# Rotary halves moved by DMA, keys and values in one product, and a scan that starts one tile earlier beside the feed-forward layer

## The chip, the core and the metric

The kernel runs on one core of a Trainium2 chip. The metric is the time of one execution on the device, in microseconds (us). A core has five engines that run their own instruction streams and meet through semaphores: PE (matrix products; its weight loads are shown as PEld), DVE (vector work), ACT (activations, and it can issue DMAs), POOL (here it issues accumulating DMAs) and SP (it issues DMAs and nothing else). 16 DMA engines serve all queues.

## The reference

One decoder layer for 4 batches of 512 positions by 512 features, all in float32: attention with 16 query heads over 2 key/value heads, then a state-space block (Mamba) on a context of 256 features whose output is gated by the layer-normed x, then a feed-forward layer with 8 experts' low-rank adapters, 2 picked per position.

```python
q = rope((x @ wq.T + bq).reshape(b, l, 16, 32)); k = rope((x @ wk.T + bk).reshape(b, l, 2, 32))
v = (x @ wv.T + bv).reshape(b, l, 2, 32)
# rope: x1, x2 = halves of a head's 32; [x1*cos - x2*sin, x2*cos + x1*sin]
x = x + softmax(causal(q @ k.T * scale)) @ v @ wo.T          # x was layer-normed
xi = silu(conv4(in_proj(ctx)) + conv_b)                      # 512 channels
dt_low, B, C = split(x_proj(xi)); dt = softplus(dt_proj(dt_low) + dt_b)
for l in positions:                                          # 16 states per channel
    state = state * exp(dt[l] * A) + dt[l] * xi[l] * B[l];  y[l] = state @ C[l]
x = x + (y + D * xi) * silu(layernorm(x))
# feed-forward, 1408 wide: base product, and the same with each picked expert's adapters
h0 = silu(g) * u;  hk = silu(g + g_lora_k) * (u + u_lora_k);  out = h0 @ Wd.T + sum_k w_k * (hk @ Ad_k.T @ Bd_k.T)
```

## The kernel before, in words

Features or channels lie on the 128 partitions and positions along the row, 512 wide, so a channel block is one 128x512 tile. The batches are a software pipeline: while PE computes the feed-forward layer of batch t, DVE and ACT run the scan of batch t+1, and the attention of t+1 follows. All orders are written out in the program; each engine runs its block (`@block.tensor`, `@block.vector`, ...) as one stream. A pass over one batch has these stages:

- **Head**: output of attention, gate, normalisation, router, masks; beside them the convolution of the next batch and its x-projection (`project_x`, L711), which ACT copies to xdt_sb (`split_first`, L508) and stores to DRAM as bc_rows, the rows of B and C. ACT then starts y_sb with D*u (L516).
- **Evaluations** (33 of them, `EVAL`): for each of 11 tiles f of the feed-forward width a base product (`base`, L858: eight 128x512 products) and two adapter steps (`add_slot`, L870), each followed by ACT's silu (L642) and DVE's product with the up half (L1211), then `down_adapters` (L878). The small products that make dt (`project_dt`, L720) and their softplus (L522) sit beside evaluations 2 and 3 (`DT_SLOTS`); the normalisation of the next batch's x (L982, L992) sits at evaluations 1 and 3 (`NORM_AT`).
- **Down stage** (11 slots): the down product (L938, four 128x512 products a slot) on PE, and beside it the projections of the next batch (`project`). Query tile n is projected at slot n+1 (L746), moved by ACT to q_raw (L570), turned by a product with a constant matrix (`rot`, L753), and DVE forms raw*cos + turned*sin in three instructions (`rotate`, L1054, L1057, L1061) at slot n+2. Tile 4 is the keys, stored once for each of four row groups. The values come after it, by four products of their own (L760), an ACT move (L576), four transposes (L767) and one copy (L1066).
- **Attention** (32 steps, L784 on PE: two heads by 128 queries a step).

The scan of one batch is cut in 49 pieces on DVE (`scan_piece`): "du", and for each of 16 states "mul" (L1035), "run" (the scan itself, L1040) and "out" (L1045), all over 128x2048. A table (`plan`) deals them to slots: 29 pieces in the evaluations, 20 in the down stage, none in the attention of batches 1 to 3. For each state ACT makes a decay (`make_decay`, L548, four exponentials), ACT issues the broadcast load bc_sb (L538), and POOL adds the result to y_sb by a DMA (L461). Decays and B/C rows are double buffered, so state n waits for state n-2. q_raw is double buffered as well: ACT moves tile n only when DVE has finished tile n-2.

Batch 0 has no feed-forward layer beside it: its projections run alone, with one scan piece in each of 11 slots, and the rest of its scan lies in its attention.

## Time and profile before

| | us |
|---|---|
| median of 3 runs | 1518.23 (1510.87 to 1524.1) |
| the profiled execution | 1524.03, its span 1522.2 |
| PE busy | 1368.4 (90%) |
| DVE busy | 1021.4 (67%) |
| ACT busy | 701.7 (46%) |

The span is what the trace covers; the profiled execution's own time is 1.8 us longer. A pass over a batch in the middle repeats every 351.6 us, three times. Busy shares are means over stages that have different limits, so the sections below read single stretches. In rows of the trace a number in brackets is the time in which the engine stood idle just before, with what it waited for; "issue" there means that the trace shows no wait. Matmul rows count two records for one float32 product.

### The profile page before, as it was taken

The numbers are of one execution on the slowest core, as the hardware profiler recorded it, in microseconds if no ns is written. First come the engines' busy times: TensorE is split into PE (matmuls) and PEld (weight loads), VectorE is DVE, ScalarE is ACT, GpSimd is POOL, SyncE is SP. The second block draws the span as 40 slices with busy tenths as digits, with TensorE's granted clock in tenths as the row PEclk, the third lists the DMA queues.
The fourth block names the chain that finished last, engine by engine and source line by source line (L and its number), as shares of the span: only waits on it lengthen the run. The fifth ranks groups of instructions, "written<-read, shape, count | busy, mean of one in ns | idle before, by whom it ended". The sixth has DMA issues, their size and how long they took to land.

```text
span 1522.2 us, 15997 instructions
## 1 busy us (share of the span) xinstructions
PE 1368.4 (90%) x5768; PEld 673.0 (44%) x5768; DVE 1021.4 (67%) x1203; ACT 701.7 (46%) x1490; POOL 89.6 (6%) x116
## 2 busy tenths in 40 slices
PE   6747777999999899899999799899999799799999
PEld 2324444444444465444444365444444355444443
DVE  4799996578989645669898744748988944511110
ACT  5445653365542385365552276455553177211110
POOL 0000001000000000000000000100000000100000
PEclk8955569999999699999999689999999879699999
DMA  5376661147767600127766700126766620011202
GB/s 200 70 191 147 137 141 31 41 121 176 187 151 170 152 2 2 44 72 183 186 162 156 188 11 2 42 64 151 188 162 159 154 67 2 0 31 52 62 31 83
DMA packets 53277, 158.80 MB, mean 104 GB/s; under 512 B 5072, under 2 KB 10704, under 8 KB 44752
## 3 DMA queue, kind: packets, MB, share of 16 engines
q0 software_dynamic: 9216, 67.11, 22.1%
q1 hardware_dynamic: 25664, 54.23, 10.8%
q10 hardware_dynamic: 18320, 36.45, 8.5%
q8 instruction: 47, 0.77, 0.2%
q14 instruction: 30, 0.25, 0.0%
HBM read 86.20 MB, written 4.46 MB: 60 GB/s over the span
## 4 chain that ended last, share of the span: by engine, by line
PE 66%; DVE 21%; ACT 6%; issue 4%; DMA 3%; ACTq 0%; DVEq 0%; POOL 0%
PE ps_a L858 21%; PE ps_a L870 9%; DVE state L1040 8%; PE ps_a L938 5%; PE ps_b L878 5%; PE ps_a L784 5%; PE ps_w L837 4%; PE ps_b L798 3%; DVE state L1035 3%; PE ps_w L746 3%; DMA y_sb<-state 3%; DVE state L1045 3%; PE ps_w L904 2%; ACT r L590 2%; DVE neg_max L1075 2%
## 5 line engine op out<-in xcount | busy, mean ns | idle before, releaser
L858 PE MATMUL ps_a<-xt,w_sb 128*128 128x512 f32 x704 | 320.0, 609 | 6.4 <-DVE r L1211 6.4
L1040 DVE TENSOR_TENSOR_SCAN state<-decay,state 128x2048 f32<-128x2048 f32 x64 | 282.7, 4417 | 2.1
L1211 DVE TENSOR_TENSOR r<-r,ps_a 128x512 f32<-128x512 f32 x132 | 90.2, 685 | 189.3 <-ACT r L642 189.3
L858 PEld LDWEIGHTS ps_a<-xt,w_sb 128*128 128x128 f32 x704 | 137.0, 196 | 180.8 <-issue 180.8
L642 ACT ACTIVATE r<-ps_a 128x512 f32<-128x512 f32 x132 | 78.4, 596 | 268.2 <-PE ps_a L858 122.7
L590 ACT ACTIVATE r<-ps_a,neg_max 128x128 f32<-128x128 f32 (+3 forms) x256 | 134.1, 539 | 121.4 <-DVE neg_max L1075 116.0
L784 PE MATMUL ps_a<-r 32*128 32x512 f32 (+3 forms) x512 | 137.0, 620 | 51.6 <-ACT r L590 34.2
L548 ACT ACTIVATE decay<-dt_sb,decay_rate 128x511 f32<-128x511 f32 x256 | 163.2, 710 | 18.3 <-DVE state L1040 17.9
L870 PE MATMUL ps_a<-r,wb_sb 128*128 128x512 f32 x352 | 166.2, 595 | 4.5 <-DVE r L1211 2.2
L938 PE MATMUL ps_a<-wd_sb,r 128*128 128x512 f32 x352 | 163.3, 616 | 0.0
L1035 DVE TENSOR_TENSOR state<-du_sb,bc_sb 128x2048 f32<-128x2048 f32 x64 | 146.1, 2283 | 9.0 <-DMA bc_sb<-bc_rows 5.2
L1045 DVE TENSOR_TENSOR state<-state,bc_sb 128x2048 f32<-128x2048 f32 x64 | 146.4, 2287 | 1.7
L1075 DVE TENSOR_REDUCE neg_max<-ps_a 128x2 f32<-128x256 f32 (+3 forms) x128 | 104.7, 819 | 44.3 <-PE ps_a L787 42.3
L798 PE MATMUL ps_b<-cst,r 128*128 128x128 f32 x640 | 117.1, 325 | 15.2 <-ACT r L602 7.8
L938 PEld LDWEIGHTS ps_a<-wd_sb,r 128*128 128x128 f32 x352 | 70.5, 201 | 89.0 <-issue 86.0
L870 PEld LDWEIGHTS ps_a<-r,wb_sb 128*128 128x128 f32 x352 | 66.3, 190 | 90.2 <-issue 85.1
L461 POOL DMA_DIRECT2D y_sb<-state x64 | 55.8, 873 | 748.6 <-DVE state L1045 668.1
L798 PEld LDWEIGHTS ps_b<-cst,r 128*128 128x128 f32 x640 | 87.5, 171 | 22.1 <-issue 18.6
L878 PE MATMUL ps_b<-r,ad_sb 128*128 128x512 f32 x176 | 87.6, 622 | 2.9 <-DVE r L1211 2.9
L784 PEld LDWEIGHTS ps_a<-r 32*128 32x128 f32 x512 | 49.4, 235 | 85.7 <-ACT r L590 46.5
L1088 DVE TENSOR_TENSOR r<-ps_w,r 128x128 f32<-128x128 f32 x64 | 18.4, 287 | 78.1 <-ACT r L609 78.1
L602 ACT ACTIVATE xt<-ps_b 128x256 f32<-128x256 f32 (+1 forms) x128 | 57.9, 504 | 24.0 <-PE ps_b L798 23.4
(117 smaller groups left out, 1392.9 us busy)
## 6 DMA issues: line engine op xcount, KB each, us to landing
y_sb<-state POOLq DMA_DIRECT2D x64, 1024.0 KB, 9.5
bc_sb<-bc_rows ACTq DMA_DIRECT2D x64, 512.0 KB, 5.4
w_sb<-in_w_tiles SPq DMA_DIRECT2D x44, 512.0 KB, 8.0
wd_sb<-in_w_down SPq DMA_DIRECT2D x44, 256.0 KB, 3.2
wb_sb<-in_w_adapt SPq DMA_DIRECT2D x44, 128.0 KB, 2.1
xa<-in_x SPq DMA_DIRECT2D x4, 1024.0 KB, 5.2
out_x<-xb SPq DMA_DIRECT2D x16, 256.0 KB, 8.1
xn_att<-in_ctx_t SPq DMA_DIRECT2D x4, 512.0 KB, 7.8
```

The costliest lines, as they stand in the source:

```text
L548: nc.scalar.activation(decay[:, n % 2, j, 1:L], dt_sb[:, j, 1:L], ACT.Exp, scale=decay_rate[:, j, n:n + 1]).then_inc(decay_ready, 1)
L590: nc.scalar.activation(probs[:, (2 * s + k) % 4, 0:(i + 1) * P], score_place(s, k), ACT.Exp, bias=neg_max[:, s % 2, k:k + 1], accum_out=ro ...
L784: nc.tensor.matmul(score_place(s, k), q_t[rows, m, i * P:(i + 1) * P], k_t[rows, 0:width], start=True, stop=False, tile_position=(rows.sta ...
L798: mm = nc.tensor.transpose(ps_b[:, k, kt * P:(kt + 1) * P], probs[:, (2 * s + k) % 4, kt * P:(kt + 1) * P], ident)
L858: mm = nc.tensor.matmul(ps_a[:, 2 * (f % 2) + half, :], w_sb[:, slot, at + k * P:at + (k + 1) * P], xt[:, k, :], start=(k == 0), stop=Fals ...
L870: mm = nc.tensor.matmul(ps_a[:, 2 * (f % 2) + half, :], wb_sb[:, f % 2, at:at + P], low[:, 2 * half + k - 1, :], start=False, stop=(k == 2 ...
L878: mm = nc.tensor.matmul(ps_b[:, k - 1, :], ad_sb[:, f, :], hk[:, (2 * f + k - 1) % 4, :], start=(f == 0), stop=(f == FT - 1), skip_group_c ...
L938: mm = nc.tensor.matmul(ps_a[:, i, :], hb[:, f, i * P:(i + 1) * P], wd_sb[:, f % 2, :], start=(f == 0), stop=False, skip_group_check=True)
L1035: tt(state[:, n % 2, :, :], du_sb[:], row, ALU.mult).then_inc(scan_chain, 1)
L1040: nc.vector.tensor_tensor_scan(flat, decay[:, n % 2, :, :].rearrange("p j l -> p (j l)"), flat, 0.0, ALU.mult, ALU.add).then_inc(scan_chai ...
L1045: tt(state[:, n % 2, :, :], state[:, n % 2, :, :], row, ALU.mult).then_inc(scan_chain, 1)
L1075: nc.vector.tensor_reduce(neg_max[:, s % 2, :], both, AX.X, ALU.max, negate=True)\
```

## The change

Two things change together.

**Keys, values and rotation.** The constant matrix and its five products go. After ACT has moved a tile to q_raw, SP issues eight DMAs of 16 rows each that write its swapped halves to q_rot (`rotate` in SP's block), and the table of sines now carries the sign. Keys and values come from one product, tile 0 (wkv_sb, rows of keys and values in turn); the queries are tiles 1 to 4. The key rows are copied to their second places by two DMAs. The four value transposes follow at slot 3 and DVE copies the values out in four instructions at slot 4. The four value products and ACT's move of them go.

**The scan.** The dt products and softplus move from evaluations 2 and 3 to 0 and 1, "du" and "mul 0" from evaluation (1,1) to (0,1), and so every later piece of the evaluations by one tile. 32 pieces lie in the evaluations, 17 in the down stage. The start of y_sb moves from ACT to DVE (`begin_y`), the normalisation to evaluations 0, 1 and 3, and decay 0 is made at the slot of "du", behind the softplus.

```diff
-NORM_AT = {EVAL_AT[0, 1]: (0, 1), EVAL_AT[0, 2]: (2, 3)}
-DT_SLOTS = (2, 3)
+NORM_AT = {EVAL_AT[0, 0]: (0, 1), EVAL_AT[0, 1]: (2,), EVAL_AT[0, 2]: (3,)}
+DT_SLOTS = (0, 1)
...
-        slots[between(at["du", 0] if n < 2 else at["run", n - 2], at["run", n])]["decay"].append(n)
+        slots[at["du", 0] if n == 0 else between(at["du", 0] if n == 1 else at["run", n - 2], at["run", n])]["decay"].append(n)
...
-IN_EVALS = [0 if f == 0 else ((0, 2, 0) if f == 1 else (0, 2, 1))[k] for f, k in EVAL]
-IN_DOWN = 20
+IN_EVALS = [({EVAL_AT[0, 1]: 2}.get(e, 0) if f == 0 else (0, 2, 1)[k]) for e, (f, k) in enumerate(EVAL)]
+IN_DOWN = 17
...
+VALUES_AT = 3
+COPY_AT = 8
 def projections(f):
     raw = f - 1 if 1 <= f <= TILES else None
-    back = f - 2 if 2 <= f <= TILES + 1 else None
-    return raw, back, {TILES + 2: 0, TILES + 3: 1}.get(f)
+    turned = f - 2 if 2 <= f <= TILES + 1 else None
+    return raw, turned
...
+            raw = projections(f)[0]
+            names += [("raw", raw)] * (raw is not None) + [("vt", 0)] * (f == VALUES_AT)
...
+        q_rot = r2[:, 6:8, :]
...
+            def rotate(b, n):
+                bank, count = use(("raw", n), b)
+                sp.wait_ge(work_free[bank], count + 1)
+                for p in range(0, P, HD):
+                    for to, of in ((p, p + HD // 2), (p + HD // 2, p)):
+                        sp.dma_start(q_rot[to:to + HD // 2, n % 2, :], q_raw[of:of + HD // 2, n % 2, :])\
+                            .then_inc(rot_loaded[n % 2], 16)
+            def copy_keys(b):
+                sp.wait_ge(qk_ready, b * TILES + 1)
+                for p in (0, 2 * HD):
+                    sp.dma_start(k_t[p + HD:p + 2 * HD, :], k_t[p:p + HD, :]).then_inc(k_copied, 16)
+            def beside_down(b, f):
+                if 0 <= f - 3 < TILES:
+                    rotate(b, f - 3)
+                if f == COPY_AT:
+                    copy_keys(b)
             def ffn_loads(t):
                 for f in range(2, FT):
                     load_w(t, f)
                     load_wb(t, f)
                 for f in range(FT):
                     load_wd(t, f)
+                    if t + 1 < BATCH:
+                        beside_down(t + 1, f)
...
+            for n in range(TILES):
+                rotate(0, n)
+            copy_keys(0)
...
-                act.wait_ge(u_ready, b * JT + JT)
-                for j in range(JT):
-                    nc.scalar.activation(y_sb[:, j, :], u_sb[:, j, :], ACT.Identity,
-                                         scale=vec[:, V_D + j:V_D + j + 1]).then_inc(y_init, 1)
             def softplus(b, tiles):
...
-                        act.wait_ge(dt_ready, b + 1)
+                        for j in (JT - 2, JT - 1):
+                            bank, count = use(("dt", j), b)
+                            act.wait_ge(work_free[bank], count + 1)
...
+                    if n == 2:
+                        of, turned = use(("vt", 0), b)
+                        act.wait_ge(work_full[of], turned + 1)
+                    bias = q_bias[:, n - 1:n] if n > 0 else vec[:, V_BKV:V_BKV + 1]
                     nc.scalar.activation(q_raw[:, n % 2, :], ps_w[:, bank, :], ACT.Identity, bias=bias,
-                                         scale=SCALE if n < MT else 1.0).then_inc(work_free[bank], 1)
-                if projections(f)[2] == 0:
-                    act.wait_ge(v_full, b + 1)
-                    act.wait_ge(qk_ready, b * TILES + TILES)
-                    nc.scalar.activation(q_raw[:, 0, :], ps_b[:, 0, :], ACT.Identity,
-                                         bias=vec[:, V_BV:V_BV + 1]).then_inc(v_moved, 1)
+                                         scale=SCALE if n > 0 else 1.0).then_inc(work_free[bank], 1)
...
-            for f in range(FT):
-                if f == 0:
-                    transposed("att", "xt", 0, False)
+            load_bc(0, PLAN_FIRST[DOWN])
+            make_decay(0, PLAN_FIRST[DOWN])
+            transposed("att", "xt", 0, False)
+            project(0, 0)
+            for f in range(1, FT):
...
-                    scan_inputs(t + 1, PLAN_NEXT[e])
+                    load_bc(t + 1, PLAN_NEXT[e])
                     softplus(t + 1, [j for _, j in dt_uses(e)])
+                    make_decay(t + 1, PLAN_NEXT[e])
...
-                raw, back, values = projections(f)
+                raw = projections(f)[0]
                 if raw is not None:
                     if raw == 0:
                         xt_moved("xt", b, False)
                     bank = fill(pe, ("raw", raw), b)
                     for k in range(KT):
-                        w = wq_sb[:, k, raw * P:(raw + 1) * P] if raw < MT else wk_sb[:, k, :]
+                        w = wq_sb[:, k, (raw - 1) * P:raw * P] if raw > 0 else wkv_sb[:, k, :]
                         mm = nc.tensor.matmul(ps_w[:, bank, :], w, xt[:, k, :], start=(k == 0), stop=(k == KT - 1))
                     mm.then_inc(work_full[bank], 1)
-                if back is not None:
-                    bank = fill(pe, ("back", back), b)
-                    raw_bank, raw_count = use(("raw", back), b)
+                if f == VALUES_AT:
+                    raw_bank, raw_count = use(("raw", 0), b)
                     pe.wait_ge(work_free[raw_bank], raw_count + 1)
-                    nc.tensor.matmul(ps_w[:, bank, :], rot, q_raw[:, back % 2, :], start=True, stop=True)\
-                        .then_inc(work_full[bank], 1)
-                if values == 0:
-                    if not first_batch(b):
-                        pe.wait_ge(down_ready, b)
-                    for k in range(KT):
-                        mm = nc.tensor.matmul(ps_b[:, 0, :], wv_sb[:, k, :], xt[:, k, :],
-                                              start=(k == 0), stop=(k == KT - 1))
-                    mm.then_inc(v_full, 1)
-                if values == 1:
-                    pe.wait_ge(v_moved, b + 1)
+                    bank = fill(pe, ("vt", 0), b)
                     for i in range(NT):
-                        mm = nc.tensor.transpose(ps_b[:, 0, i * P:(i + 1) * P], q_raw[:, 0, i * P:(i + 1) * P], ident)
-                    mm.then_inc(v_turned, 1)
+                        mm = nc.tensor.transpose(ps_w[:, bank, i * P:(i + 1) * P], q_raw[:, 0, i * P:(i + 1) * P], ident)
+                    mm.then_inc(work_full[bank], 1)
             def attention(b, slots):
                 pe.wait_ge(qk_ready, (b + 1) * TILES)
-                pe.wait_ge(v_ready, b + 1)
+                pe.wait_ge(k_copied, 32 * (b + 1))
+                pe.wait_ge(v_ready, NT * (b + 1))
...
+            def begin_y(b):
+                dve.wait_ge(u_ready, b * JT + JT)
+                for j in range(JT):
+                    ts(y_sb[:, j, :], u_sb[:, j, :], vec[:, V_D + j:V_D + j + 1], None, ALU.mult).then_inc(y_init, 1)
+            def normalize_next(t, e):
+                for i in NORM_AT.get(e, ()):
+                    dve.wait_ge(loaded["x"], 16 * t + 32)
+                    deviation("att", t + 1, xa, i)
+                for i in NORM_AT.get(e, ()):
+                    scaled("att", t + 1, xa, xn_att, i)
...
-                total = TILES
-                _, n, values = projections(f)
+                n = projections(f)[1]
                 if n is not None:
                     raw_bank, raw_count = use(("raw", n), b)
                     dve.wait_ge(work_free[raw_bank], raw_count + 1)
                     tt(rope_tmp, q_raw[:, n % 2, :], cos_t, ALU.mult).then_inc(rope_chain, 1)
-                    bank = filled(dve, ("back", n), b)
-                    part = q_t[:, n, :] if n < MT else k_t
-                    tt(part, ps_w[:, bank, :], sin_t, ALU.mult).then_inc(work_free[bank], 1)
-                    dve.wait_ge(rope_chain, b * total + n + 1)
-                    bank, count = use(("back", n), b)
-                    dve.wait_ge(work_free[bank], count + 1)
+                    of_parity = (TILES + 1 - n % 2) // 2
+                    dve.wait_ge(rot_loaded[n % 2], 16 * 2 * (P // HD) * (b * of_parity + n // 2 + 1))
+                    part = q_t[:, n - 1, :] if n > 0 else k_t
+                    tt(part, q_rot[:, n % 2, :], sin_t, ALU.mult).then_inc(rope_chain, 1)
+                    dve.wait_ge(rope_chain, 2 * (b * TILES + n + 1))
                     tt(part, part, rope_tmp, ALU.add).then_inc(qk_ready, 1)
-                    dve.wait_ge(qk_ready, b * total + n + 1)
-                if values == 1:
-                    dve.wait_ge(v_turned, b + 1)
-                    nc.vector.tensor_copy(v_sb[:], ps_b[:, 0, :].rearrange("p (i d) -> p i d", i=NT)[:, :, 0:VD])\
-                        .then_inc(v_ready, 1)
+                    dve.wait_ge(qk_ready, b * TILES + n + 1)
+                if f == VALUES_AT + 1:
+                    bank = filled(dve, ("vt", 0), b)
+                    turned = ps_w[:, bank, :].rearrange("p (i g c d) -> p i g c d", i=NT, g=KV_HEADS, c=2)
+                    for i in range(NT):
+                        copied = nc.vector.tensor_copy(v_sb[:, i, :].rearrange("p (g d) -> p g d", g=KV_HEADS),
+                                                       turned[:, i, :, 1, :])
+                        copied.then_inc(v_ready, 1)
+                    dve.wait_ge(v_ready, NT * (b + 1))
+                    nc.vector.tensor_copy(scrap[:], ps_w[0:1, bank, 0:1]).then_inc(work_free[bank], 1)
...
             normalize("att", 0, xa, xn_att)
+            begin_y(0)
...
+                begin_y(t + 1)
+                normalize_next(t, 0)
                 for e in range(1, EVALS):
                     evaluate(t, e)
-                    for i in NORM_AT.get(e, ()):
-                        dve.wait_ge(loaded["x"], 16 * t + 32)
-                        deviation("att", t + 1, xa, i)
-                    for i in NORM_AT.get(e, ()):
-                        scaled("att", t + 1, xa, xn_att, i)
+                    normalize_next(t, e)
...
-    c[:, C_SIN:C_SIN + L] = np.sin(ang)
+    c[:, C_SIN:C_SIN + L] = np.where(p % HD < half, -1.0, 1.0).astype(np.float32)[:, None] * np.sin(ang)
...
+    def keys_values(k, v):
+        return np.concatenate([part[g * HD:(g + 1) * HD] for g in range(KV_HEADS) for part in (k, v)])
```

ACT, first evaluations of a batch in the middle, before (L508 the copy to xdt_sb, L516 the start of y_sb, L522 softplus, L548 decays, L642 the silu of an evaluation, r2 the gate):

```order
L508 ACTIVATE xdt_sb<-ps_b 128x512
L513 DMA bc_rows<-xdt_sb 32x512
L516 ACTIVATE y_sb<-state,vec 128x512 x4
L642 ACTIVATE r2<-ps_a 128x512 x2
L522 ACT_TABLE_LOAD
L522 ACTIVATE dt_sb<-ps_w,vec 128x512 x2
L642 ACT_TABLE_LOAD
L642 ACTIVATE r2<-ps_a 128x512
L522 ACT_TABLE_LOAD
L522 ACTIVATE dt_sb<-ps_w,vec 128x512 x2
L642 ACT_TABLE_LOAD
L642 ACTIVATE r2<-ps_a 128x512
```

And now (softplus is L542, decays L566, silu L657):

```order
L533 ACTIVATE xdt_sb<-ps_b 128x512
L538 DMA bc_rows<-xdt_sb 32x512
L542 ACT_TABLE_LOAD
L542 ACTIVATE dt_sb<-ps_w,vec 128x512 x2
L657 ACT_TABLE_LOAD
L657 ACTIVATE r2<-ps_a 128x512
L554 DMA bc_sb<-bc_rows 128x2x512 x2
L542 ACT_TABLE_LOAD
L542 ACTIVATE dt_sb<-ps_w,vec 128x512 x2
L566 ACT_TABLE_LOAD
L566 ACTIVATE decay<-dt_sb,decay_rate 128x511 x4
L657 ACT_TABLE_LOAD
```

The four instructions on y_sb are gone, softplus and the first decay stand between the first silus.

SP, the down stage of a batch in the middle, now (before, eleven rows of wd_sb stood there with nothing between):

```order
L412 DMA wd_sb<-in_w_down 128x512 x4
L419 DMA r2<-r2 16x512 x8
L412 DMA wd_sb<-in_w_down 128x512
L419 DMA r2<-r2 16x512 x8
L412 DMA wd_sb<-in_w_down 128x512
L419 DMA r2<-r2 16x512 x8
```

Each group of eight waits for ACT's move of its tile, and the weight loads behind it wait with it.

DVE, the start of the down stage, now (L1239 ends the weighing of the adapters, L1058 is the scan itself, L1063 and L1053 "out" and "mul", L1071 to L1077 the rotation):

```order
L1239 TENSOR_TENSOR r1<-r2 128x512
L1058 SCALAR_TENSOR_TENSOR state<-decay,state 128x2048
L1063 TENSOR_TENSOR state<-state,bc_sb 128x2048
L1053 TENSOR_TENSOR state<-du_sb,bc_sb 128x2048
L1071 TENSOR_TENSOR r2<-r2,cst 128x512
L1075 TENSOR_TENSOR r2<-r2,cst 128x512
L1077 TENSOR_TENSOR r2<-r2 128x512
L1058 SCALAR_TENSOR_TENSOR state<-decay,state 128x2048
L1063 TENSOR_TENSOR state<-state,bc_sb 128x2048
```

Three scan pieces instead of four stand ahead of the first rotation, and L1075 now waits for DMAs, where it waited for a product.

## Rows read from the trace of the kernel before

**Rows 1.** Busy time by stage, a middle batch: start:end, length, busy by engine, clock, DMA.
```profile
588.00:940.00 352.00, 329.67 (x1468) 162.12 (x1458) 256.22 (x300) 182.32 (x378) 22.34 (x28) 0.94 0.43 109
```

**Rows 2.** The chain of waits over the whole span: start us, us, what.
```profile
698.91 6.87 PE ps_a L858 x16
710.92 6.87 PE ps_a L858 x16
```

**Rows 3.** The chain of waits, end of the same batch's down stage.
```profile
860.68 1.21 DVE xb L1224 x2
862.03 0.79 PE ps_a L784 x4
```

**Rows 4.** Timeline of ACT, first evaluations: start us, us, what, idle before.
```profile
644.11 0.60 ACT L508 ACTIVATE xdt_sb<-ps_b 128x512 f32<-128x512 f32 x1 [6.19 <-PE ps_b L711]
645.18 2.56 ACT L516 ACTIVATE y_sb<-state,vec 128x512 f32<-128x512 f32 x4 [0.48 <-ACT xdt_sb L508]
...
655.57 1.26 ACT L522 ACTIVATE dt_sb<-ps_w,vec 128x512 f32<-128x512 f32 x2
...
669.30 2.56 ACT L548 ACTIVATE decay<-dt_sb,decay_rate 128x511 f32<-128x511 f32 x4
671.88 1.28 ACT L642 ACT_TABLE_LOAD   x1
673.17 1.08 ACT L642 ACTIVATE r<-ps_a 128x512 f32<-128x512 f32 x2
```

**Rows 5.** Timeline of PE, the same evaluations.
```profile
674.63 7.11 PE L858 MATMUL ps_a<-xt,w_sb 128*128 128x512 f32 x16 [2.13 <-DVE r L1211]
```

**Rows 6.** Timeline of DVE, the same evaluations.
```profile
648.25 0.69 DVE L1211 TENSOR_TENSOR r<-r,ps_a 128x512 f32<-128x512 f32 x1 [6.11 <-ACT r L642]
```

**Rows 7.** Timeline of DVE, the down stage.
```profile
783.18 0.69 DVE L1216 TENSOR_TENSOR r<-ps_b,r 128x512 f32<-128x512 f32 x1 [1.36 <-PE ps_b L878]
...
785.12 4.42 DVE L1040 TENSOR_TENSOR_SCAN state<-decay,state 128x2048 f32<-128x2048 f32 x1
789.57 2.29 DVE L1045 TENSOR_TENSOR state<-state,bc_sb 128x2048 f32<-128x2048 f32 x1
...
801.42 0.69 DVE L1057 TENSOR_TENSOR r<-ps_w,cst 128x512 f32<-128x512 f32 x1 [2.22 <-PE ps_w L753]
...
809.14 0.69 DVE L1057 TENSOR_TENSOR r<-ps_w,cst 128x512 f32<-128x512 f32 x1 [1.11 <-PE ps_w L753]
...
848.26 0.40 DVE L1066 COPY v_sb<-ps_b 128x256 f32<-128x256 f32 x1
...
851.51 2.29 DVE L1035 TENSOR_TENSOR state<-du_sb,bc_sb 128x2048 f32<-128x2048 f32 x1 [0.66 <-DMA y_sb<-state]
```

**Rows 8.** Timeline of PE, the down stage.
```profile
790.06 3.60 PE L746 MATMUL ps_w<-xt,wq_sb 128*128 128x512 f32 x8
...
842.82 1.11 PE L767 MATMUL ps_b<-cst,r 128*128 128x128 f32 x4 [3.68 <-ACT r L576]
```

**Rows 9.** DMA issues of the whole span: KB each, median us to landing.
```profile
y_sb<-state POOLq DMA_DIRECT2D x64, 1024.0 KB, 9.5
bc_sb<-bc_rows ACTq DMA_DIRECT2D x64, 512.0 KB, 5.4
wd_sb<-in_w_down SPq DMA_DIRECT2D x44, 256.0 KB, 3.2
...
bc_rows<-xdt_sb ACTq DMA_DIRECT2D x4, 64.0 KB, 1.6
```

**Rows 10.** SP's issues of line 410: duration of one in ns, min/median/max.
```profile
L410 SPq DMA_DIRECT2D wd_sb<-in_w_down x44: 327/328/433, 404.3 to 1508.7; - x44
```

**Rows 11.** Busy time, two groups of eight attention steps (columns of rows 1).
```profile
862.00:883.60 21.60, 21.32 (x114) 11.08 (x114) 8.46 (x18) 12.80 (x44) 0.00 (x0) 0.50 0.65 183
895.20:911.70 16.50, 15.98 (x208) 10.05 (x204) 8.24 (x21) 14.71 (x54) 0.00 (x0) 1.00 0.01 2
```

**Rows 12.** Timeline of DVE, batch 0, the first "mul".
```profile
43.92 2.29 DVE L1035 TENSOR_TENSOR state<-du_sb,bc_sb 128x2048 f32<-128x2048 f32 x1 [5.18 <-DMA bc_sb<-bc_rows]
```

More of the change, by code:

```diff
@@ L279, in decoder_layer @@
         qk_ready = sem("qk_ready")
-        v_full = sem("v_full")
-        v_moved = sem("v_moved")
-        v_turned = sem("v_turned")
+        rot_loaded = [sem(f"rot_loaded{k}") for k in range(2)]
+        k_copied = sem("k_copied")
         v_ready = sem("v_ready")
@@ L1280, in constant_table @@
     half = HD // 2
-    for m in range(P):
-        if m % HD < half:
-            c[m + half, C_ROT + m] = -1.0
-        else:
-            c[m - half, C_ROT + m] = 1.0
     c[:, C_MASK:C_MASK + P] = np.where(p[None, :] <= p[:, None], 0.0, NEG)
-    for k in range(32, P):
-        c[k, C_SEL + k % 32] = 1.0
     inv = (np.float32(10000.0) ** (-np.arange(half, dtype=np.float32) / np.float32(half))).astype(np.float32)
@@ L1343 @@
         "wq": rows(a["L0_attn_wq"][heads].T),
-        "wk": rows(a["L0_attn_wk"][kv_rows].T),
-        "wv": rows(np.tile(a["L0_attn_wv"].T, (1, P // VD))),
+        "wkv": rows(keys_values(a["L0_attn_wk"], a["L0_attn_wv"]).T),
         "wo": rows(a["L0_attn_wo"][:, heads].T),
```

31 lines of the change are left out of this document (10 added, 21 removed).

## The prediction, made before the changed kernel ran

> **What bounds the kernel now.** I read the windows by stage first, then the chain of waits, then the timelines of the engines where the chain changes hands. In a middle batch PE is busy 330 of 352 us and DVE 256 [rows 1]. The chain says where each of them counts. In the evaluations it is PE: the base product of one tile starts 12.01 us after that of the tile before [rows 2], which is 14 products at 6.87/8 = 0.86 us, with nothing between. In the down stage PE's own work is some 80 products, but the end is DVE's: its last scan piece ends at 860.7, the sums of the output follow, and only then does the first attention product start, at 862.03 [rows 3]. So a PE product taken out of the down stage is worth nothing by itself; a scan piece taken out is worth its duration, if DVE does not wait instead. Two PE stalls stand out: 2.13 us ahead of the third base product, for ACT and DVE [rows 5], and 3.68 us for the values' move [rows 8], which DVE's longer path hides. Attention starts at granted clock 0.50, which is 1.2 GHz, and later steps have 1.00, 2.4 GHz [rows 11].
>
> **The change, part by part.** I use the middle batch's times; batches 1 to 3 repeat it.
>
> *Evaluations.* After ACT's copy to xdt_sb ends at 644.7, it lost 2.56 us on y_sb [rows 4]. Now it goes: load 1.28, two softplus 1.26 (647.3), load, silu 0.60 (649.2), load, softplus (651.7), load 1.28, decay 2.56 (655.6), load (656.9) [rows 4]. PE meanwhile does two dt products, an adapter step, two dt products (0.86 each, 6 in all) and the base product of 6.87: 644.8 + 5.2 + 6.9 = 656.9. So the next silu is ready when its product is, and PE is not held. The second decay, which with its two table loads had kept the silu from PE (669.3 to 673.2 [rows 4]), now stands one tile earlier and behind three silus that are done by then, ahead of a base product of 6.87 us that covers its 1.28 + 2.56 + 1.28 = 5.1. The 2.13 us stall goes: -2.1 a batch; bounds +2 (a stall at the new place) and -2.9 (0.7 more for the dt products that fill PE's first wait). DVE takes four instructions for y_sb, at most 0.69 each by the nearest row, 2.8 in all, in a wait of 6.11 us [rows 6]; without that cover they would delay an evaluation by as much. The three more pieces lie in tiles 0 and 1, where DVE had only the evaluations. From tile 2 on both kernels have three pieces a tile: 4.42 + 2 x 2.25 plus three evaluations of 0.69 is 11.0 of 12.0 us, unchanged.
>
> A row shows 1.28 us for a table load, and the activation after it starts 0.01 us later [rows 4]. The Trainium skill (ScalarE: Activation LUTs, "What ACT_TABLE_LOAD costs") puts a switch at 2.66 us, with a drain of 1.38 behind the load. By it the silu above, behind five loads, would come 6.9 us later, and the evaluations would lose about 4.5 us a batch, not gain 2.1. The trace disagrees, so I don't use it.
>
> *Down stage, pieces.* 20 pieces (7 scans, 13 products) become 17 (6 and 11): 4.42 + 2 x 2.25 = -8.9 us on DVE's path [rows 7]. The values cost four small copies and a one-element copy where one of 0.40 was [rows 7]: +0.8 (between 0 and 1.6).
>
> *Down stage, waits.* DVE waited 2.22 + 1.11 + 0.66 = 4.0 us in the stage [rows 7]. The new wait is for the swapped halves. Let d be the time from ACT's move to their landing. SP issues eight, 0.33 to 0.43 us each [rows 10], so 2.6 to 3.5. A 64 KB DMA lands in 1.6, a 256 KB one on SP's own queue beside this stage's traffic in 3.2 [rows 9]. So d lies between 4.2 and 6.7; I take 2.9 + 2.4 = 5.3. Tile 0's product still ends at 793.7 [rows 8], its move at 794.3, the halves land at 799.6. DVE, after weighing (783.2 to 785.1) and three pieces (8.9), stands at the rotation at 794.7: it waits 4.9. Rotation 2: ACT moves tile 2 only after issuing the load of B and C for state 13, which waits for "out 11"; DVE then has a rotation, a "mul" and 0.65 to do (4.9), and ACT's move and d come to 6.8, so 1.9. Rotations 1, 3 and 4 have two or more pieces of cover. At the end, "mul 15" waits for POOL's addition of state 13, 9.5 us [rows 9], against 8.9 of DVE's work: 0.6. Together 7.4 instead of 4.0, +3.4. Sum of the stage: -8.9 + 0.8 + 3.4 = **-4.7**; with d = 4.2 it is -6.9, with d = 6.7 it is -1.9.
>
> *Down stage, PE and SP.* PE loses nine products (7.7 us) and its 3.68 wait, and is done near 843, twelve us before DVE: nothing. Weight loads for slots 4 to 8 now wait behind rotations; each is issued one to two slots (3.4 to 6.9 us) ahead of its use and lands in 3.2 [rows 9]: nothing, or under 1 us of PE time that DVE hides. The two key copies land before DVE is through.
>
> *Attention.* PE still idles ahead of it, so it starts at the lower clock as now: 0. *Last batch's feed-forward layer:* untouched.
>
> *Batch 0.* ACT's 2.56 us ahead of softplus go, and "mul 0" waited 5.18 us for rows that are now asked for earlier [rows 12]; against it, decay 0 (1.28 + 2.56) stands ahead of the moves of xt, and rotation 0 waits for d. I take -2.3, between 0 and -4.
>
> Sum: 3 x (-2.1 - 4.7) - 2.3 = **-22.7 us**. The profiled execution is 1524.0, so 1501.3 for one like it; it is the slowest of the three, and against the median of 1518.2 the forecast is 1495.5, rounded to **1496 us**.
>
> **The rivals.**
>
> *The eight DMAs land one after the other (slower).* Then d = 8 x 1.6 = 12.8 [rows 9]. Rotations 0, 2 and 4 wait 12.4, 9.4 and 4.9, with 0.6 at the end 27.3: the stage becomes 15 us longer, a batch 13; with +6 in batch 0 the time is 1518 + 39 + 6 = 1563. It decides from d of about 9. For it: they are small, on one queue, and share the engines with POOL's additions. Against it: SP's issue times [rows 10] don't show one waiting for the last. The Trainium skill (DMA: Bandwidth & Descriptors, "Rules for kernel authors") speaks for it: transfers to disjoint groups of partitions serialize, and those under 64 KB are mostly overhead. Chance 0.08.
>
> *The traffic slows them part of the way.* d = 8: waits of 7.4, 4.4 and 0.6 eat what the three pieces give, the evaluations' 2.1 stays: 1518 - 6 = 1512. The spread of landings on SP's queue speaks for some of it. Chance 0.16.
>
> *The clock comes back sooner.* Eight attention steps take 21.6 us at 0.50 and 16.5 at 1.00 [rows 11]. If PE, whose stage is now shorter and without the 3.68 us gap, gets the higher clock from the start, each of three batches gains 5 more: 1496 - 15 = 1481. Against it: DVE still ends last and PE idles even longer. Chance 0.10.
>
> *The clock stays low through an attention.* The three other groups of eight steps would cost 5 us each, 15 a batch, 45 in all: 1541. It starts just as before, so 0.04.
>
> **How the numbers follow.** The forecast has 0.62. Its own range is 1484 to 1508: d between 4.2 and 6.7 is -7 to +8 us, batch 0 and the evaluations add 4, and the three runs spread by 13. The range reaches up to the half-slowed case and down to the clock case: 1480 to 1514. This kernel's measurement tells 1% from no change, 15 us. Faster needs 1503 or less: most of the forecast (0.55) and the clock case (0.10), 0.65. Within 1%: the rest of the forecast (0.07), the half-slowed case (0.16) and a little of the others, 0.25. Slower: 0.10.
>
> **What would show it.** In the new profile: no idle row of 2 us ahead of the third base product; 3 us less from one weighing to the next product of attention for each missing scan piece, less a DVE wait on q_rot's DMA of about 5 us at rotation 0 and 2 at rotation 2; eight issues on SP of 0.35 us; PE idle 12 us ahead of attention at clock 0.50. I am wrong if DVE waits more than 7 us at rotation 0, if rotations 1 or 3 wait too, or if the silus of tiles 0 and 1 hold PE.

## The result: slower by 1.1%

| | before | after |
|---|---|---|
| median of 4 runs, us | 1520.89 (1510.87 to 1524.1) | 1536.86 (1533.05 to 1539.21) |
| profiled execution, its span | 1524.03, 1522.2 | 1533.05, 1531.4 |

The ratio is 1.0114, interval 1.006 to 1.0168. The forecast was 1496 us. Between the two profiled executions the 9.2 us of span divide so (each batch cut where ACT copies xdt_sb, where DVE begins to weigh, at its first output sum L1245, and at the second sum; us):

| stage | before, batches 1, 2, 3 | after | forecast a batch | measured, in all |
|---|---|---|---|---|
| evaluations | 139.0, 139.1, 139.1 | 136.7, 136.7, 136.6 | -2.1 | -7.2 |
| down stage | 77.5, 77.4, 77.5 | 84.6, 83.4, 83.3 | -4.7 | +18.8 |
| attention | 98.4, 98.4, 97.3 | 96.9, 96.3, 95.6 | 0 | -5.3 |
| head | 37.2, 36.8, 36.8 | 35.5, 36.8, 35.5 | 0 | -2.9 |
| batch 0, once | 255.3 | 261.8 | -2.3 | +6.5 |
| behind the last second sum | 212.6 | 211.8 | 0 | -0.8 |

The chain of waits, same batch as before. Where [rows 2] has only PE and [rows 3] DVE's scan, the down stage now passes through SP's issues and the landing of the halves.

```profile
705.16 6.87 PE ps_a L864 x16
...
717.18 6.87 PE ps_a L864 x16
...
799.34 0.70 ACT r L591
800.62 1.38 SPq L419
...
806.85 2.91 DMA r<-r
809.78 0.70 DVE r L1075
...
853.55 9.74 DMA y_sb<-state
...
872.48 2.40 DVE xb L1245 x4
```

DVE in the down stage (start, duration, what, in brackets the idle time before): tiles 0, 2 and 4 wait, tile 3 (838.70) and tile 1 do not.

```profile
809.78 0.69 DVE L1075 TENSOR_TENSOR r<-r,cst 128x512 f32<-128x512 f32 x1 [9.03 <-DMA r<-r]
...
829.22 0.69 DVE L1075 TENSOR_TENSOR r<-r,cst 128x512 f32<-128x512 f32 x1 [6.38 <-DMA r<-r]
830.67 0.62 DVE L1084 COPY v_sb<-ps_w 128x64 f32<-128x64 f32 x4
831.32 0.14 DVE L1088 COPY scrap<-ps_w 1x1 f32<-1x1 f32 x1
...
838.70 0.68 DVE L1075 TENSOR_TENSOR r<-r,cst 128x512 f32<-128x512 f32 x1
...
849.42 0.69 DVE L1075 TENSOR_TENSOR r<-r,cst 128x512 f32<-128x512 f32 x1 [1.84 <-DMA r<-r]
...
863.31 2.29 DVE L1053 TENSOR_TENSOR state<-du_sb,bc_sb 128x2048 f32<-128x2048 f32 x1 [1.06 <-DMA y_sb<-state]
```

The waits are 9.03 + 6.38 + 1.84 + 1.06 = 18.3 us where [rows 7] had 4.0: +14.3. The pieces give back 8.9 and the value copies add 0.76 - 0.40. That is +5.8; the stage grew by 6.0.

SP's issues of the five rotations, each of eight DMAs, and POOL's additions of scan results:

```profile
800.05 7.38 SPq L419 DMA_DIRECT2D r<-r  x8
808.10 4.93 SPq L419 DMA_DIRECT2D r<-r  x8
819.23 8.55 SPq L419 DMA_DIRECT2D r<-r  x8
828.44 5.58 SPq L419 DMA_DIRECT2D r<-r  x8
839.40 8.62 SPq L419 DMA_DIRECT2D r<-r  x8
```
```profile
798.24 0.87 POOL L486 DMA_DIRECT2D y_sb<-state  x1 [11.78 <-DVE state L1063]
818.31 0.86 POOL L486 DMA_DIRECT2D y_sb<-state  x1 [19.20 <-DVE state L1063]
838.48 0.86 POOL L486 DMA_DIRECT2D y_sb<-state  x1 [19.31 <-DVE state L1063]
```

An undisturbed rotation takes SP 4.93 us, 0.62 for each DMA, not the 0.33 to 0.43 of [rows 10]. The rotations of tiles 0, 2 and 4 begin 1 to 2 us behind an addition of 1 MB, and take 7.4 to 8.6. DVE gets their halves 11.5, 10.9 and 10.9 us after the addition's issue; the additions land after 8.6, 9.9 and 9.8 us, so the last halves are there 2.9, 1.0 and 1.1 us behind the landing. Tile 0 comes there by PE's pace, and its halves also stand behind the load of B and C that ACT issued at 799.35: it took 9.1 us, and they come 1.3 us after it. For tiles 2 and 4 it is no chance: their move stands on ACT behind the load of B and C, which waits for the same "out" that releases the addition:

```profile
818.51 0.69 ACT L591 ACTIVATE r<-ps_w,q_bias 128x512 f32<-128x512 f32 x1 [11.62 <-DVE state L1063]
```

PE, which the forecast had done 12 us before DVE, ends with it; only 1.50 us of idling remain ahead of attention, where 5.57 stood before. It waits 5.14 us until DVE's value copies free a bank of ps_w, 6.87 us for a weight load that SP issued behind tile 4's rotation, and 2.91 us for one that SP issued at 857.48 with no rotation ahead of it. That one took 6.3 us and landed 0.5 us behind the addition of 853.55. The last row of the second block is the window of the first 21.6 us of attention (columns of [rows 1]): clock 0.60 where [rows 11] had 0.50.

```profile
831.52 1.22 PE L764 MATMUL ps_w<-xt,wq_sb 128*128 128x512 f32 x1 [5.14 <-DVE scrap L1088]
...
851.13 9.74 PE L944 MATMUL ps_a<-wd_sb,r 128*128 128x512 f32 x16 [6.87 <-DMA wd_sb<-in_w_down]
863.79 5.11 PE L944 MATMUL ps_a<-wd_sb,r 128*128 128x512 f32 x8 [2.91 <-DMA wd_sb<-in_w_down]
...
873.83 0.49 PE L790 MATMUL ps_a<-r 32*128 32x128 f32 x4 [1.50 <-DVE xb L1245]
```
```profile
wd_sb<-in_w_down SPq DMA_DIRECT2D x1, 256.0 KB, 6.3
...
873.80:895.40 21.60, 20.71 (x124) 11.23 (x125) 8.67 (x20) 13.40 (x46) 0.00 (x0) 0.60 0.65 183
```

Batch 0 on DVE: the wait of [rows 12] fell from 5.18 to 1.80 us (at 34.39), and four longer ones stand behind it. The first of them, for the move behind decay 0, is in scan_only too (6.92 us), whose batch 0 is shorter than before's.

```profile
43.56 0.69 DVE L1071 TENSOR_TENSOR r<-r,cst 128x512 f32<-128x512 f32 x1 [6.88 <-ACT r L591]
49.95 0.69 DVE L1075 TENSOR_TENSOR r<-r,cst 128x512 f32<-128x512 f32 x1 [5.69 <-DMA r<-r]
71.56 0.69 DVE L1075 TENSOR_TENSOR r<-r,cst 128x512 f32<-128x512 f32 x1 [5.93 <-DMA r<-r]
95.48 2.29 DVE L1053 TENSOR_TENSOR state<-du_sb,bc_sb 128x2048 f32<-128x2048 f32 x1 [4.72 <-DMA y_sb<-state]
```

### The profile page after: what moved, and what is told of

Its sections match the earlier page's. It is cut to its first block, busy times and chain, and to the rows that moved or that the text cites. A ratio compares the mean times of both kernels' runs of the same rounds, so it can differ in the third digit from the quotient of the medians.

```text
span 1531.4 us, 15999 instructions
## 1 busy us (share of the span) xinstructions
PE 1331.7 (87%) x5696; PEld 652.9 (43%) x5696; DVE 1030.1 (67%) x1235; ACT 693.8 (45%) x1473; POOL 89.2 (6%) x116
## 4 chain that ended last, share of the span: by engine, by line
PE 63%; DVE 18%; ACT 6%; SPq 5%; DMA 5%; issue 3%; ACTq 0%; POOL 0%; DVEq 0%
PE ps_a L864 20%; PE ps_a L876 10%; DVE state L1058 7%; SPq L419 5%; PE ps_b L884 5%; PE ps_a L790 4%; PE ps_a L944 4%; PE ps_w L843 4%; PE ps_b L804 3%; DMA y_sb<-state 3%; DVE state L1063 3%; DVE state L1053 2%; PE ps_w L910 2%; ACT r L605 2%; DMA r<-r 2%
## 5 line engine op out<-in xcount | busy, mean ns | idle before, releaser
L1058 DVE TENSOR_TENSOR_SCAN state<-decay,state 128x2048 f32<-128x2048 f32 x64 | 282.8, 4418 | 1.8
L864 PEld LDWEIGHTS ps_a<-xt,w_sb 128*128 128x128 f32 x704 | 136.2, 194 | 171.8 <-issue 171.4
L944 PE MATMUL ps_a<-wd_sb,r 128*128 128x512 f32 x352 | 170.1, 638 | 30.5 <-DMA wd_sb<-in_w_down 30.5
L657 ACT ACTIVATE r<-ps_a 128x512 f32<-128x512 f32 x132 | 78.8, 597 | 257.5 <-PE ps_a L876 138.0
L790 PE MATMUL ps_a<-r 32*128 32x512 f32 (+3 forms) x512 | 130.0, 590 | 58.8 <-ACT r L605 45.5
L566 ACT ACTIVATE decay<-dt_sb,decay_rate 128x511 f32<-128x511 f32 x256 | 163.4, 711 | 35.9 <-DVE state L1058 35.5
L1053 DVE TENSOR_TENSOR state<-du_sb,bc_sb 128x2048 f32<-128x2048 f32 x64 | 146.2, 2284 | 10.2 <-DMA y_sb<-state 8.1
L1063 DVE TENSOR_TENSOR state<-state,bc_sb 128x2048 f32<-128x2048 f32 x64 | 146.5, 2289 | 1.8
L876 PEld LDWEIGHTS ps_a<-r,wb_sb 128*128 128x128 f32 x352 | 66.6, 191 | 88.5 <-issue 83.3
L764 PE MATMUL ps_w<-xt,wq_sb 128*128 128x512 f32 x128 | 66.7, 671 | 32.4 <-DVE scrap L1088 22.5
L790 PEld LDWEIGHTS ps_a<-r 32*128 32x128 f32 x512 | 46.0, 219 | 91.8 <-ACT r L605 57.6
## 6 DMA issues: line engine op xcount, KB each, us to landing
wd_sb<-in_w_down SPq DMA_DIRECT2D x44, 256.0 KB, 3.0
out_x<-xb SPq DMA_DIRECT2D x16, 256.0 KB, 8.0
```

Source lines behind the costliest of these rows:

```text
L566: nc.scalar.activation(decay[:, n % 2, j, 1:L], dt_sb[:, j, 1:L], ACT.Exp, scale=decay_rate[:, j, n:n + 1]).then_inc(decay_ready, 1)
L790: nc.tensor.matmul(score_place(s, k), q_t[rows, m, i * P:(i + 1) * P], k_t[rows, 0:width], start=True, stop=False, tile_position=(rows.sta ...
L864: mm = nc.tensor.matmul(ps_a[:, 2 * (f % 2) + half, :], w_sb[:, slot, at + k * P:at + (k + 1) * P], xt[:, k, :], start=(k == 0), stop=Fals ...
L876: mm = nc.tensor.matmul(ps_a[:, 2 * (f % 2) + half, :], wb_sb[:, f % 2, at:at + P], low[:, 2 * half + k - 1, :], start=False, stop=(k == 2 ...
L944: mm = nc.tensor.matmul(ps_a[:, i, :], hb[:, f, i * P:(i + 1) * P], wd_sb[:, f % 2, :], start=(f == 0), stop=False, skip_group_check=True)
L1053: tt(state[:, n % 2, :, :], du_sb[:], row, ALU.mult).then_inc(scan_chain, 1)
```

## The experiments

Every ratio is to the kernel before, measured beside it on the same chip. "Stage" is the middle batch's down stage: 77.4 us before, 83.4 after.

### Which half of the change costs

**scan_only**: the kernel before with the scan part alone (the slots of dt, normalisation and decay 0, `IN_DOWN = 17`, y_sb by DVE). **rot_only**: the changed kernel with that part undone.

```diff
...
-IN_DOWN = 20
+IN_DOWN = 17
...
```

> The kernel before with only the scan part of the change (dt products beside the first evaluations, 17 pieces left, y_sb begun on DVE); keys, values and rotation as before. My theory (the DMAs of the rotation cost what the scan part gives): the evaluations lose their 2.1 us stall, the down stage loses 8.9 us of pieces less 1 to 5 us of longer waits for the turning product, so 6 to 10 us a batch: 1490 to 1502. Rival (moving three pieces to the front costs as much as it gives, and the rotation is innocent): 1515 to 1530.

Measured 1495.92 us, ratio 0.9863 (0.984 to 0.9887); batch 0 250.9, stage 74.9. Evaluations 136.2. Of the 8.9 us of pieces DVE gives 6.2 back as waits, 10.2 us where there were 4.0:

```profile
787.01 0.69 DVE L1070 TENSOR_TENSOR r<-ps_w,cst 128x512 f32<-128x512 f32 x1 [6.31 <-PE ps_w L754]
802.46 0.69 DVE L1070 TENSOR_TENSOR r<-ps_w,cst 128x512 f32<-128x512 f32 x1 [2.25 <-PE ps_w L754]
834.83 2.29 DVE L1048 TENSOR_TENSOR state<-du_sb,bc_sb 128x2048 f32<-128x2048 f32 x1 [1.64 <-DMA y_sb<-state]
```

> The changed kernel with the scan as before (29 pieces in the evaluations, 20 in the down stage, dt products at evaluations 2 and 3, y_sb begun on ACT, the old order of batch 0). My theory: rotations 0 and 2 wait about 9 and 6 us less the one more piece that stands before them, PE and the weight loads are late as in the changed kernel, so 4 to 9 us a batch more than before and 5 to 9 in batch 0: 1537 to 1556. Rival (it is the scan part that costs): within 8 us of before, 1512 to 1528.

Measured 1549.13 us, 1.0219 (1.0191 to 1.0248); stage 87.9, batch 0 260.9. So the scan part is the gain, and the other part, rotation by DMA with keys and values in one product, the loss. kv_turned below tells these two apart.

### Taking the DMAs away, and making them one

**no_swap_dma**: the changed kernel without the eight DMAs; DVE multiplies q_raw, halves not swapped, by the sines, so q and k lack the swap.

```diff
...
-                        sp.dma_start(q_rot[to:to + HD // 2, n % 2, :], q_raw[of:of + HD // 2, n % 2, :])\
-                            .then_inc(rot_loaded[n % 2], 16)
...
-                    tt(part, q_rot[:, n % 2, :], sin_t, ALU.mult)
+                    tt(part, q_raw[:, n % 2, :], sin_t, ALU.mult)
```

> The changed kernel without the forty DMAs a batch: DVE multiplies q_raw itself by the sines, so the halves are not swapped, and nothing on SP stands between the weight loads. My theory: the waits of 9.0, 6.4 and 1.8 us on DVE go, and the PE waits for weights go; ACT still moves tile 2 only after a scan piece. 12 to 18 us a batch less than the changed kernel's down stage and about 10 in batch 0: 1475 to 1492. Rival (the waits are taken over by the next thing, DVE's order and ACT's): above 1505.

Measured 1477.89 us, 0.9749 (0.973 to 0.9768); stage 67.4, batch 0 250.7. By the ratios (1.0114 and 0.9749) the eight DMAs of a tile and the waits for them are worth 3.65% of the time, some 55 us. **one_copy**: one DMA of all 128 rows in their place, halves not swapped either.

```diff
...
+                sp.dma_start(q_rot[:, n % 2, :], q_raw[:, n % 2, :]).then_inc(rot_loaded[n % 2], 16)
```

> The changed kernel with one plain 128-row DMA from q_raw to q_rot for each tile instead of eight 16-row ones; the halves are copied, not swapped. If the issue of eight DMAs one after the other is what makes the halves late (5.0 to 8.6 us of it), the wait at rotation 0 falls from 9.0 to about 3 us, at rotation 2 to 1 or less: 1485 to 1500. If a DMA's landing amid the additions' and the broadcast's traffic is what is late, little changes: 1525 to 1540.

Measured 1523.38 us, 1.0024 (0.9991 to 1.0058); stage 81.7, near the second forecast. With 0.5 us of issue in place of 4.9 to 8.6, DVE still waits, and its halves still come 9.5, 10.9 and 10.7 us behind the addition's issue:

```profile
800.55 0.69 DVE L1072 TENSOR_TENSOR r<-r,cst 128x512 f32<-128x512 f32 x1 [6.98 <-DMA r<-r]
...
819.93 0.69 DVE L1072 TENSOR_TENSOR r<-r,cst 128x512 f32<-128x512 f32 x1 [6.32 <-DMA r<-r]
...
839.88 0.69 DVE L1072 TENSOR_TENSOR r<-r,cst 128x512 f32<-128x512 f32 x1 [1.59 <-DMA r<-r]
```
```profile
791.06 0.87 POOL L483 DMA_DIRECT2D y_sb<-state  x1 [11.79 <-DVE state L1060]
809.07 0.86 POOL L483 DMA_DIRECT2D y_sb<-state  x1 [17.14 <-DVE state L1060]
829.18 0.86 POOL L483 DMA_DIRECT2D y_sb<-state  x1 [19.25 <-DVE state L1060]
```

So the number of DMAs is the smaller part of the loss here. The Trainium skill (DMA: Bandwidth & Descriptors, "Rules for kernel authors") advises one 128-partition transfer over two to disjoint halves of the partitions, since these serialize. Here one transfer in place of eight gained 0.9% by the ratios and did not remove the wait.

### Taking the traffic away

**small_add**: POOL's additions move 16 of 2048 columns; the rest of the sum is left out. **small_rows**: the loads of B and C after the first two move 16 of 512 columns.

```diff
-                    pool.dma_start(y_sb[:].rearrange("p j l -> p (j l)"),
+                    pool.dma_start(y_sb[:].rearrange("p j l -> p (j l)")[:, 0:16],
```

> The changed kernel in which POOL's DMA adds only 16 of the 2048 columns of each state to y_sb (the rest of the sum is left out), so its 1 MB stream is gone. If that stream is what stretches the issue of the eight DMAs from 5 to 7.4 and 8.6 us and delays their landing, rotations 0, 2 and 4 issue in about 5 us and the halves are there 7 us after the move: waits at rotations 0 and 2 fall from 9.0 and 6.4 to about 6 and 3.5; with the additions' own waits gone too, 1500 to 1515. If it is the rows of B and C, the waits stay at 8 or more and the time above 1518.

Measured 1506.62 us, 0.9926 (0.9904 to 0.9947); stage 73.2. All five rotations are issued in 4.93 to 5.29 us, and the waits are 5.65, 2.70 and 0:

```profile
795.83 0.69 DVE L1075 TENSOR_TENSOR r<-r,cst 128x512 f32<-128x512 f32 x1 [5.65 <-DMA r<-r]
...
811.59 0.69 DVE L1075 TENSOR_TENSOR r<-r,cst 128x512 f32<-128x512 f32 x1 [2.70 <-DMA r<-r]
```

That is nearly the forecast (4.9 and 1.9; stage 77.4 - 4.7 = 72.7). For a down stage without additions the forecast would have been nearly right.

> The changed kernel in which the broadcast of the B and C rows moves only 16 of 512 columns after the first two states (the rest of the rows is stale, so the sums are not the reference's). If the broadcast, issued by ACT in the same microsecond as the move, is what stretches the issues, they take about 5 us and the waits at rotations 0 and 2 fall to 6 and 3.5: 1500 to 1515. If it is the additions, nothing moves: 1528 to 1540.

Measured 1522.6 us, 1.0029 (1.0008 to 1.0049); stage 79.2, waits 7.77, 5.51 and 0.95: between the two forecasts. Beside additions the issues still take 7.06 to 7.76 us. So it is the addition that stretches the issue, and the loads of the rows add about 1 us to each wait.

### Moving the issue

**move_first**: ACT's `project` ahead of `load_bc`, so that the move does not wait with the addition.

```diff
-                    load_bc(t + 1, PLAN_NEXT[DOWN + f])
                     project(t + 1, f)
+                    load_bc(t + 1, PLAN_NEXT[DOWN + f])
```

> The changed kernel with ACT's move of a projected tile ahead of the load of the B and C rows in each slot of the down stage. My theory: tile 2 is moved when its product ends, 5 us sooner and away from the additions' burst; its eight DMAs issue in 5 us and land 7 us after, so rotation 2 waits 1 us or less instead of 6.4, and rotation 4's move at the same place comes earlier too: 5 to 8 us a batch, 1508 to 1524. Rival (the halves are late because of the traffic, whenever they are asked for; the wait goes elsewhere): 1530 to 1540.

Measured 1525.11 us, 1.0037 (1.0014 to 1.0059), 1 us above what was expected; stage 79.1. Tile 2 is issued in 4.93 us and no longer waits; tile 4 waits 1.90 beside an addition. Tile 0 waits 11.00, and no longer for the addition (issued 798.03, landed 7.5 us later). ACT now issues the load of B and C at 806.00, SP the last of tile 0's eight DMAs at 806.27, and that one lands 0.2 us behind the load, at 811.5:

```profile
bc_sb<-bc_rows ACTq DMA_DIRECT2D x1, 512.0 KB, 5.3
```

So the load that no longer holds up tile 2 now meets tile 0's halves. That it is what delays them fits the two landings, but no run takes it away here.

**two_queues**: four of the eight DMAs from ACT, behind its move.

```diff
...
+                    act.wait_ge(work_free[bank], count + 1)
+                    for p in range(P // 2, P, HD):
+                        for to, of in ((p, p + HD // 2), (p + HD // 2, p)):
+                            act.dma_start(q_rot[to:to + HD // 2, n % 2, :], q_raw[of:of + HD // 2, n % 2, :])\
...
```

> The changed kernel with four of the eight DMAs of each tile issued by ScalarE, right behind its move, and four by SyncE. Everything is computed. Theory (issuing one after another on one queue makes over half of d, 4.93 us unstretched and up to 8.6 beside the additions): the issues take 2.5 to 4.3 us, d falls by 2.5 to 4, the waits from 9.03, 6.38 and 1.84 us to about 6, 3 and 0, the down stage from 83.7 to about 76, and the time to 1505 to 1518 us. Rival (the transfers, not the issues, are late: beside the additions' packets they land when those are through): d and the waits stay within 1 us, ScalarE loses 2.5 us a tile, and the time is 1530 to 1545 us.

Measured 1522.64 us, 1.0035 (1.0006 to 1.0065); stage 81.4. Away from additions the issue is halved, 2.40 us on SP; beside them it takes 4.65 to 5.6. Tile 0's wait fell by 2.5 us, the other two did not move: their halves come 11.1 us behind the additions' issues (812.09, 832.41), where it was 10.9. The time lies between the two forecasts: each theory holds for some tiles.

```profile
803.57 0.69 DVE L1081 TENSOR_TENSOR r<-r,cst 128x512 f32<-128x512 f32 x1 [6.54 <-DMA r<-r]
...
823.16 0.69 DVE L1081 TENSOR_TENSOR r<-r,cst 128x512 f32<-128x512 f32 x1 [6.54 <-DMA r<-r]
...
843.51 0.69 DVE L1081 TENSOR_TENSOR r<-r,cst 128x512 f32<-128x512 f32 x1 [1.99 <-DMA r<-r]
```

The Trainium skill (the same page and section) says that issuing from several engines gives no bandwidth and saves only issue time. These rows agree: 4.93 against 2.40 us of issue, and the same arrival beside an addition.

### Keeping one half of the rotation part

**kv_turned**: keys and values from one product, key copies by DMA, but rotation by PE's product as before.

```diff
...
+                    nc.tensor.matmul(ps_w[:, bank, :], rot, q_raw[:, back % 2, :], start=True, stop=True)\
+                        .then_inc(work_full[bank], 1)
...
```

> The changed kernel with the rotation given back to PE: five turning products with the constant matrix, halves read from PSUM; keys and values by one product, transposed early, the key rows copied by two DMAs, the scan part as changed. My theory: the forty DMAs are the whole loss, so the rest of the change is worth what the scan part alone gave and a little for the values' four products: 1478 to 1496, at or below scan_only. Rival (keys and values first cost by themselves, since every tile is moved a slot or an order later): 1500 to 1520.

Measured 1504.57 us, 0.992 (0.9889 to 0.9951); stage about 75.5, batch 0 255.5. The rival held. It is above scan_only (stage 74.9, batch 0 250.9): four products fewer on PE gain nothing, and batch 0 loses 4.6. The two were measured at different times on different chips, each beside the kernel before. From 0.992 to the changed kernel's 1.0114 is the price of the rotation by DMA, 1.9%; from 0.9863 to 0.992, 0.6%, that of keys and values in one product.

### More distance

**pieces_first**: the changed kernel with each slot's scan pieces ahead of the tile's rotation on DVE. **pieces_first_two_queues** has four DMAs on ACT as well.

```diff
-                    rotate(t + 1, f)
+                    turn_values(t + 1, f)
                     for piece in PLAN_NEXT[DOWN + f]["dve"]:
                         scan_piece(t + 1, piece)
+                    rotate(t + 1, f)
```

> The changed kernel with one move on VectorE: in each of the ten down-stage slots the slot's scan pieces come before the turning of a tile instead of behind it (the value copies stay at the slot's start). Everything is computed. It puts two pieces or one, about 6 to 9 us, between ScalarE's move of a tile and VectorE's need of the turned halves, beside the distance there is. Theory (the loss is the latency d, about 10 us from move to landing, seen by an engine that has nothing else to do, and not the DMA traffic in itself): the waits of 9.03, 6.38 and 1.84 us at tiles 0, 2 and 4 fall below 2 us each, the down stage goes from 83.7 to 68 to 72 us a batch, and the time to 1485 to 1500 us. Rival (the weight loads of the down products, queued on SyncE behind the rotations, are the next bound, since PE waited 6.87 and 2.91 us for them): the waits of VectorE go and the stage still takes 78 us or more, 1515 us or above.

Measured 1497.23 us, 0.9876 (0.9831 to 0.9922); stage 74.0, above the expected 68 to 72. Tiles 2 to 4 wait no more. Tile 0 still does, and tile 1 now: their issues start at 781.47 and 789.58, each behind an addition (779.65, 788.84). Tile 0's last DMA (788.33) was issued 0.1 us behind a load of B and C (788.24, landed 6.8 us later) and comes 0.2 us after it, as in move_first. The expected "below 2 us each" failed there.

```profile
795.24 0.69 DVE L1075 TENSOR_TENSOR r<-r,cst 128x512 f32<-128x512 f32 x1 [6.42 <-DMA r<-r]
...
802.01 0.69 DVE L1075 TENSOR_TENSOR r<-r,cst 128x512 f32<-128x512 f32 x1 [2.42 <-DMA r<-r]
...
844.45 0.69 DVE L1247 TENSOR_TENSOR xb<-ps_a,xb 128x512 f32<-128x512 f32 x1 [0.21 <-PE ps_a L951]
```

The last row shows PE, held up by weight loads, ending just after DVE: it is the next bound, by 0.2 us.

> Both of the edits of this call to the changed kernel: pieces ahead of the turning, and four DMAs each from ScalarE and SyncE. Everything is computed. Theory (distance has covered the latency already): within 0.5% of pieces_first, since what is left to save is not waited for; SyncE reaches the weight loads 2.5 us sooner for each tile. Rival (weight loads behind the rotations are the bound): 10 us or more below pieces_first. A third case: ScalarE's 2.5 us a tile delay the decays and the moves, and it is 5 us or more above pieces_first.

Measured 1485.08 us, 0.9783 (0.9746 to 0.982); stage 70.0, batch 0 250.2. "Within 0.5%" was wrong: 12 us below, as the rival had it. But DVE's waits in the stage went from 8.8 to 5.3 us, which is most of the 4.0 that the stage gained, and batch 0 gained 5.5; the weight loads' share was not separated. The profiled executions are only 5.4 us apart, since two attentions of pieces_first's were short ones, 90.7 and 92.9 us (last section).

**turn_last**: scan_only with the pieces ahead of the turning, rotation by PE's product.

> The kernel before with the scan part of the change alone (as in scan_only, 1495.92 us) and VectorE's order within a down-stage slot turned round: the pieces first, then the tile's turning and, at their slot, the value copies. Everything is computed; rotation is still a product of TensorE. Theory (scan_only's waits of 6.31 and 2.25 us at the turning products are distance too: TensorE's product comes behind ScalarE's move, which comes behind its other work): they go, the stage falls from 74.8 to about 67 to 69 us, and the time to 1472 to 1482 us, under every kernel so far that computes everything. Rival (the turning products' chain over the two PSUM banks goes from tile to tile, so a later release of a bank only moves the wait): the time stays at 1490 to 1502 us.

Measured 1478.03 us, 0.9737 (0.9707 to 0.9768); stage 67.5, batch 0 248.8. One wait of the stage is left, 3.06 us in place of 10.2:

```profile
778.52 0.69 DVE L1070 TENSOR_TENSOR r<-ps_w,cst 128x512 f32<-128x512 f32 x1
...
785.99 0.69 DVE L1070 TENSOR_TENSOR r<-ps_w,cst 128x512 f32<-128x512 f32 x1 [3.06 <-PE ps_w L754]
```

It computes everything, beats both kernels (2.6% below before and, by the ratios, 3.7% below after), and is level with the kernel that left the swap out.

## Why the prediction was wrong

Between the profiled executions the forecast was -22.7 and the result +9.1 by the rows of the table, 31.8 us apart: 32.9 in the down stage, 8.8 in batch 0, -0.9 in the evaluations, -9.0 elsewhere. The rest of the distance to 1536.9 is that the profiled execution after lay 3.8 us below its median, where before's lay 5.8 above the median that the forecast used.

1. **Evaluations: right.** -2.4 a batch for -2.1, and no idle row of 2 us ahead of the third base product. The single load of 1.28 us for a table was the right price. The Trainium skill (ScalarE: Activation LUTs, "What ACT_TABLE_LOAD costs") has 2.66 for a switch; here the activation behind the load starts 0.02 us after it (load 653.40 to 654.68, softplus 654.70).
2. **The pieces: right** as work, -8.9 us. What they free comes back as waits unless something else fills it: in scan_only the stage gained 2.5 of 8.9, in turn_last, the same pieces in another order, 9.9.
3. **"I take 2.9 + 2.4 = 5.3": the step that failed.** From ACT's move (800.0) to DVE's start d was 9.7, then 10.0 and 10.1. Two things were in it. An issue on SP costs 0.62 us, not 0.37 (small_add: d of 6.4, inside my bounds, waits of 5.65 and 2.70); I had taken the price from weight loads that are issued one at a time. In the new kernel a weight load right behind a rotation takes 0.58 as well. And beside an addition the last halves come only after its landing, however they are issued: 1.0 to 2.9 us behind it with eight on one queue, 0.3 to 1.2 with one DMA, 0.7 to 1.5 with eight on two queues. That is 10 us of stage (73.2 to 83.4), the larger part. I had the additions' 9.5 us in [rows 9] and used them for "mul 15" alone. The 3.2 us that I read as a landing "beside this stage's traffic" are a median of 44 loads. In this very stage of the kernel before, the loads of 820.29 and 832.31 were issued 2.6 and 1.4 us behind an addition, took 7.8 and 9.0 us, and landed 0.2 us behind it. The longest of the 44 took 10.2:

   ```profile
   wd_sb<-in_w_down SPq DMA_DIRECT2D x1, 256.0 KB, 7.8
   ...
   wd_sb<-in_w_down SPq DMA_DIRECT2D x1, 256.0 KB, 9.0
   ...
   DMA to landing us min/median/max: 2.5/3.2/10.2
   ```

   What I failed to ask was when the rotation is issued: the "out" that frees the load of B and C also frees the addition, so two rotations of five always meet one, and tile 0's did here. I had even written that tile 2's move waits for "out 11".
4. **"PE and SP in the down stage: nothing": wrong.** PE waited 6.87 us for weights behind a rotation, 2.91 for weights beside an addition and 5.14 for the value copies, which I had not priced at all. The cover of twelve us was used up, though not exceeded.
5. **Batch 0: wrong**, +6.5 for -2.3. Rotations wait 5.69 and 5.93 us. Without the rotation DMAs the batch is 250.7: 11.1 us are theirs, and the rest of the change gave 4.6 there, more than I took.
6. **Attention: zero forecast, -1.8 a batch.** The clock rival was right in kind: with 1.50 us of idling ahead in place of 5.57, the first 21.6 us had clock 0.60, not 0.50. No run shows that this is all of the 1.8 us.

The rivals: "the traffic slows them" (d = 8, 1512) named the cause and had its size too small. "One after the other" had the size, decisive from d of about 9, and the wrong cause, as one_copy and two_queues show. I gave the two 0.24 together, and the range left 1563 out. (For d = 8 the two waits should read 7.6 and 4.6, by the sum that gave 4.9 and 1.9; that changes nothing.)

## What to carry to other kernels

Price a small transfer by where it will be issued in time, not by its size: look which large DMA is released by the same event, and take that one's landing as the lower bound. A median over all issues of a transfer hides the few that meet such a neighbour; read the longest, and when they were issued. Work removed from an engine is a gain only if what it then waits for is early; here a change of order with no work removed (turn_last over scan_only) gave 7 us a stage. Here small DMAs in place of a cheap product on an engine that was not the bound bought nothing and added waits.
